# Two matmul layers of a graph network in three blocks of 418 columns in place of four of 314

## The reference

```python
h = jnp.maximum(_layernorm(x, axis=-1), 0.0)
agg = jax.ops.segment_sum(h[src], dst, num_segments=N)
z = (1.0 + eps) * h + agg
z = jax.nn.relu(batch_norm(z @ W1 + b1, g1, be1))      # 512 -> 1024, statistics over the nodes
z = jax.nn.relu(batch_norm(z @ W2 + b2, g2, be2))      # 1024 -> 512
x = x + h + z
```

## Time and profile before

| | us |
|---|---|
| median of 3 runs | 1132.43 |
| lowest and highest | 1132.26 and 1136.16 |
| the profiled execution: its own time | 1133.7 |
| its span, first to last instruction | 1131.7 |
| PE busy | 1063.5 (94%) |
| ACT, DVE, POOL busy | 896.6, 871.2, 656.5 |
| mean granted TensorE clock | 0.986 of full speed |

### The profile page before, as it was taken

The page is one execution under the profiler, slowest core; times in us unless marked ns, Lnnn a source line. Parts: engine busy times, 40 slices in busy tenths (PEclk is TensorE's granted clock), DMA queues, the critical chain, the costliest instruction groups (busy, mean ns, idle before and its releaser), DMA issues.

```text
span 1131.7 us, 18418 instructions
## 1 busy us (share of the span) xinstructions
PE 1063.5 (94%) x5689; PEld 896.5 (79%) x5690; DVE 871.2 (77%) x1529; ACT 896.6 (79%) x1134; POOL 656.5 (58%) x549
## 2 busy tenths in 40 slices
PE   3676999998999999999999999999999999999897
PEld 1124889997888888888888888888888888888695
DVE  7998536535425388888898998998888888888686
ACT  5995845524513699999999999999999999999584
POOL 6765323002155486776888888888876677660217
PEclk9998999998999999999999999999999999999899
DMA  2004820301165386666666666666666666661002
GB/s 102 8 1 115 147 75 1 121 1 47 75 215 121 81 188 146 138 136 139 130 137 140 133 133 145 132 140 130 140 138 133 136 139 134 134 130 38 1 1 91
DMA packets 61086, 121.39 MB, mean 107 GB/s; under 512 B 7851, under 2 KB 18348, under 8 KB 60918
## 3 DMA queue, kind: packets, MB, share of 16 engines
q0 software_dynamic: 38048, 87.58, 38.1%
q1 hardware_dynamic: 22998, 33.32, 8.9%
HBM read 107.82 MB, written 7.80 MB: 102 GB/s over the span
## 4 chain that ended last, share of the span: by engine, by line
PE 86%; DVE 9%; ACT 2%; issue 2%; DVEq 1%; POOL 0%; ACTq 0%; POOLq 0%
PE banks L1033 12%; PE banks L1028 12%; PE banks L1029 12%; PE banks L933 10%; PE banks L1013 7%; PE banks L1050 6%; PE banks L1007 6%; PE banks L976 5%; PE banks L856 4%; PE banks L995 4%; DVE edge_counts L1688 4%; PE banks L1026 3%; PE banks L1110 2%; DVE key_onehot L1635 1%; PE banks L910 1%
## 5 line engine op out<-in xcount | busy, mean ns | idle before, releaser
L682 POOL DMA_INDIRECT gather_pq<-q_table,dst x157 | 295.4, 1882 | 56.8 <-issue 47.5
L674 POOL DMA_INDIRECT gather_pq<-p_table,src x157 | 173.5, 1105 | 138.7 <-PE banks L1013 85.5
L1028 PE MATMUL banks<-w_lo,h_hi 128*128 128x512 f32 x620 | 241.5, 390 | 0.0
L1029 PE MATMUL banks<-w_hi,h_hi 128*128 128x512 f32 x620 | 241.3, 389 | 0.0
L1033 PE MATMUL banks<-w_hi,h_lo 128*128 128x512 f32 x620 | 166.2, 390 | 0.0
L1029 PEld LDWEIGHTS banks<-w_hi,h_hi 128*128 128x128 f32 x620 | 116.4, 188 | 24.8
L1033 PEld LDWEIGHTS banks<-w_hi,h_lo 128*128 128x128 f32 x620 | 116.4, 188 | 24.2
L1984 DVE SCALAR_TENSOR_TENSOR h_full<-mish_work,banks 128x512 f32<-128x512 f32 (+1 forms) x154 | 98.5, 681 | 46.6 <-ACT mish_work L1337 43.4
L1028 PEld LDWEIGHTS banks<-w_lo,h_hi 128*128 128x128 f32 x620 | 116.5, 188 | 22.0
L2009 DVE SCALAR_TENSOR_TENSOR message<-mish_work,banks 128x1024 f32<-128x1024 f32 x78 | 95.3, 1222 | 8.7 <-ACT mish_work L1361 0.7
L1325 ACT ACTIVATE mish_work<-banks 128x1024 f32<-128x1024 f32 (+1 forms) x77 | 78.6, 1021 | 26.3 <-PE banks L1013 26.3
(11 more groups left out here) (267 smaller groups left out, 2677.5 us busy)
## 6 DMA issues: line engine op xcount, KB each, us to landing
edge_attr<-in_edge_attr_t SPq DMA_DIRECT2D x79, 128.0 KB, 3.5
x_nodes<-h_hi POOLq DMA_DIRECT2D x10, 256.0 KB, 13.3
x_nodes<-h_lo POOLq DMA_DIRECT2D x10, 256.0 KB, 7.9
p_table<-p_stage SPq DMA_DIRECT2D x10, 256.0 KB, 2.0
q_table<-agg_nodes SPq DMA_DIRECT2D x10, 256.0 KB, 3.0
gather_pq<-p_table,src POOLq DMA_INDIRECT x157, 3.9
gather_pq<-q_table,dst POOLq DMA_INDIRECT x157, 5.0
x_nodes<-in_x SPq DMA_DIRECT2D x3, 768.0 KB, 6.7
```

Of the source, the lines that this page charges most:

```text
L674: nc.gpsimd.indirect_dma_start(GP[:, 2 * j + k, :], None, p_tab[:, :], bass.IndirectOffsetOnAxis(ap=SRC[:, 2 * s + k:2 * s + k + 1], axis= ...
L682: nc.gpsimd.indirect_dma_start(GP[:, 2 * j + k, :], None, q_tab[:, :], bass.IndirectOffsetOnAxis(ap=DST[:, 2 * s + k:2 * s + k + 1], axis= ...
L1028: pe.matmul(at, h_high(s, j)[:, c, e], W2_LO[:, c, :], start=False, stop=False)
L1029: pe.matmul(at, h_high(s, j)[:, c, e], W2_HI[:, c, :], start=False, stop=False)
```

## The change

The first network's products go over 3 blocks of 418 columns (1254 in all). The update of the second network keeps 4 blocks of 314 under the names `UBLOCKS` and `UBW`. Three places depend on the number of blocks without being about width: PE's inner split of a tile's blocks becomes (0, 1) and (1, 3), where it was (0, 2) and (2, 4); ACT's `between` stands behind block `BLOCKS // 2`, now 1; `FREE`, the number of banks that are free at the start, becomes 3.

```diff
-BLOCKS = 4
-
-BW = -(-NODES // (2 * BLOCKS)) * 2
+
+
+BLOCKS, UBLOCKS = 3, 4
+BW, UBW = (-(-NODES // (2 * n)) * 2 for n in (BLOCKS, UBLOCKS))
 NW = BLOCKS * BW
-assert NODES <= NW <= NP
+assert NODES <= NW <= UBLOCKS * UBW <= NP
...
-        FREE = 4
+        FREE = BLOCKS
         MM_2 = BLOCKS * KH
         MM_PQ = MM_2 + BLOCKS * KD
         MM_UP = MM_PQ + 2 * NT
-        MM_U = MM_UP + BLOCKS * KD
+        MM_U = MM_UP + UBLOCKS * KD
...
                 for o in range(1, on):
-                    for first, end in ((0, BLOCKS // 2), (BLOCKS // 2, BLOCKS)):
+                    for first, end in ((0, 1), (1, BLOCKS)):
                         with pe.Fori(first, end) as b:
                             pe.wait_ge(mm_moved, base + BLOCKS * o + b + 1)
                             for k in range(kn):
...
-                nodes = slice(b * BW, (b + 1) * BW)
+                nodes = slice(b * UBW, (b + 1) * UBW)
...
-            for b in range(BLOCKS):
+            for b in range(UBLOCKS):
                 for o in range(KD):
```

More of the change, by code:

```diff
@@ L174, in gnn_kernel @@
         IOTA, _ = sb("iota", [P, NP])
-        XWORK_0, _ = sb("mish3_work_0", [P, 2, BW], at=iota_at)
-        XWORK_1, _ = sb("mish3_work_1", [P, 2, BW], at=b2_at)
+        XWORK_0, _ = sb("mish3_work_0", [P, 2, UBW], at=iota_at)
+        XWORK_1, _ = sb("mish3_work_1", [P, 2, UBW], at=b2_at)
         XWORK = (XWORK_0[:, :, :], XWORK_1[:, :, :])
@@ L323, in gnn_kernel @@
         W3B_HI, W3B_LO = W3_HI[:, 0, :, :], W3_LO[:, 0, :, :]
[L324 to L327, removed]
+        UP_0, _ = sb("u_part_0", [P, 6, UBW], at=wa_at + 4 * KD * DIM)
+        UP_1, _ = sb("u_part_1", [P, 6, UBW], at=wb_at + 4 * KD * DIM)
+        UP_2, _ = sb("u_part_2", [P, 4, UBW], at=rows_at)
+        assert 4 * 6 * UBW <= 4 * KD * DIM and 4 * 4 * UBW <= 4 * 3 * DIM
         UT, _ = sb("u_t", [P, KD, NP], at=t1_at)
@@ L745, in u_high @@
                 b, q = n // UPAIRS, n % UPAIRS
-                at = (slice(2 * q, 2 * q + 2), slice(b * BW, (b + 1) * BW))
+                at = (slice(2 * q, 2 * q + 2), slice(b * UBW, (b + 1) * UBW))
                 pool.wait_ge(u_ready, n + 1)
@@ L757, in _ @@
             pool.wait_ge(tr_done, TR_AG + NT)
-            for n in range(UPAIRS * BLOCKS):
+            for n in range(UPAIRS * UBLOCKS):
                 u_high(n)
@@ L1023, in z2 @@
                     else:
-                        pe.wait_ge(up_moved, BLOCKS * KD)
+                        pe.wait_ge(up_moved, UBLOCKS * KD)
                     pe.wait_ge(h_hi, s + 1)
@@ L1082, in _ @@
                         pe.wait_ge(up_moved, n - 3)
-                    u_terms(Z2[:, n % 4, 0:BW], W3A_HI, W3A_LO, HT_HI, HT_LO, o, b)
+                    u_terms(Z2[:, n % 4, 0:UBW], W3A_HI, W3A_LO, HT_HI, HT_LO, o, b)
                     if n in Z1_BEHIND:
@@ L1103, in y_product @@
                     pe.wait_ge(y_moved, nt - 3)
-                nodes = slice(nt * P, min((nt + 1) * P, NW))
-                last_block = (nodes.stop - 1) // BW
+                nodes = slice(nt * P, min((nt + 1) * P, UBLOCKS * UBW))
+                last_block = (nodes.stop - 1) // UBW
                 for k in range(KD):
@@ L1114, in u_product @@
             def u_product(b, q):
-                pe.wait_ge(ag_lo, -(-(b + 1) * BW // P))
+                pe.wait_ge(ag_lo, -(-(b + 1) * UBW // P))
                 if b > 0:
@@ L1120, in u_product @@
                 for o in (2 * q, 2 * q + 1):
-                    u_terms(Z2[:, o, 0:BW], W3B_HI, W3B_LO, AG_HI, AG_LO, o, b)
+                    u_terms(Z2[:, o, 0:UBW], W3B_HI, W3B_LO, AG_HI, AG_LO, o, b)
             def ag_t(nt):
@@ L1134, in _ @@
             ag_t(9)
-            for b in range(1, BLOCKS):
+            for b in range(1, UBLOCKS):
                 for q in range(UPAIRS):
@@ L1396, in _ @@
                         act.wait_ge(rows_used, 2 * NT)
-                    nc.scalar.activation(u_part(b, o)[:, 0, :], Z2[:, n % 4, 0:BW], ACT.Identity, bias=COLS[:, CB3 + o:CB3 + o + 1]).then_inc(up_moved, 1)
+                    nc.scalar.activation(u_part(b, o)[:, 0, :], Z2[:, n % 4, 0:UBW], ACT.Identity, bias=COLS[:, CB3 + o:CB3 + o + 1]).then_inc(up_moved, 1)
                     for s, first in enumerate(Z1_BEHIND):
@@ L1469, in _ @@
             u_inverse(0)
-            for n in range(1, UPAIRS * BLOCKS):
+            for n in range(1, UPAIRS * UBLOCKS):
                 u_mish(n)
@@ L2098, in u_at @@
                 b, q = n // UPAIRS, n % UPAIRS
-                return slice(2 * q, 2 * q + 2), slice(b * BW, (b + 1) * BW)
+                return slice(2 * q, 2 * q + 2), slice(b * UBW, (b + 1) * UBW)
             def u_start(n):
@@ L2105, in u_start @@
                 dve.wait_ge(mm_done, MM_U + KD * b + 2 * q + 2)
-                nc.vector.tensor_tensor(UT[:, o, nodes], Z2[:, o, 0:BW], u_part(b, 2 * q, 2), ALU.add).then_inc(u_bias, 1)
+                nc.vector.tensor_tensor(UT[:, o, nodes], Z2[:, o, 0:UBW], u_part(b, 2 * q, 2), ALU.add).then_inc(u_bias, 1)
             def u_bound(n):
@@ L2160, in _ @@
             ag_low(9)
-            for n in range(2, UPAIRS * BLOCKS):
+            for n in range(2, UPAIRS * UBLOCKS):
                 u_end(n - 2)
```

## The result

The change makes the kernel slower: 1150.39 us median of 3 runs (1148.62 to 1150.61), against 1132.43, so 18.0 us more by the medians. The forecast was 1147.1, range 1141 to 1152. The profiled execution took 1150.39 us, with a span of 1148.3, 16.6 more than that of before (which lay 1.3 us above the median of its own kernel).

The account below looks back on a forecast made before the run. PE, busy 94% of the span, was taken to bound the kernel. Savings of 1.4 and 1.3 us against losses of 0.1, 10.1, 4.8 and 2.4 gave +14.7 on 1132.43, so 1147.1 us, range 1141 to 1152.

Parts of the forecast that it names:

- handover, first three k of product 2: Start of product 2, tile 0: DVE sets the pace, so no saving, and ACT's wider last move adds 0.1 us.
- Three new waits: Product 2, tiles 0 to 2: PE's transposes wait 3.35 us each for ACT's apply behind block 0, +10.1 us.
- The clock: Behind each new wait in product 2 the granted clock falls to half for one stretch, 1.6 us each, +4.8.
- The saving: Fewer, wider matmuls save fixed cost: 1.4 us in product 1 and 1.3 in product 2.
- 384 matmuls at 144.5 ns become 288 at 187.7: Product 1: 55.5 us of matmuls become 54.1, a saving of 1.4 us.
- the second point of the line: 512-column matmuls at 226.6 ns; with 314 columns they gave 0.415 ns per column plus 14, so 187.7 at 418.
- The 0.5 us that was estimated by the 2.5 ns: Products 1 and 2: alternative saving from 192 fewer matmuls at the skill's fixed cost; not used in the sum.
- The late end of DVE: End of product 2: ten layer-norm statistics make DVE 2.2 us late for the last block; last apply +2.4 us.
- What costs nothing: Three banks, fewer DVE and ACT operations, and the unchanged update add nothing; one possible bank wait up to 1 us.
- The bank wait of product 1: Product 1, near 181.5 us: 1 us of cover expected; a wait showing there would be a sign of error.
- The sum: Whole kernel: -1.4 - 1.3 + 0.1 + 10.1 + 4.8 + 2.4 = +14.7 us, giving 1147.1.

Follow-up runs that it names:

- e1: Changed kernel with product 2's transposes behind the first two of three blocks; 1135.87 us, ratio 1.002 to the kernel before.
- e2: Kernel before, four blocks of 314, with product 2's transposes behind the first block alone; 1148.11 us, ratio 1.0116.
- e12: Changed kernel with twelve further DVE operations ahead of the edge loop and nothing else; 1149.32 us, ratio 1.0144.
- e3: Changed kernel with 14 unread matmuls ahead of each of three transpose groups inside product 2; 1147.3 us, ratio 1.0119.
- e6: Kernel before with unread matmuls in its own waits, around the last transposes, ahead of P and at the edge attributes; 1130.47 us, ratio 0.9967.
- e5: Three blocks, transposes behind two, columns left out or repeated to vary matmul width; only start distances read, 145.3 ns at 314 columns, 216.7 at 480.
- e11: Three blocks with transposes behind two, late layer-norm statistics, filled waits and twelve more DVE operations, against the kernel before; 1130.69 us, ratio 0.9976.

## Why the prediction was right or wrong

Against the profiled execution of before, the 16.6 us of span are made up so (the rows add up to 16.5, each being rounded):

| from where to where | forecast | measured |
|---|---|---|
| start of product 1 | 0 | +0.4 |
| matmuls of product 1 | -1.4 | -0.2 |
| handover, first three k of product 2 | +0.1 | +0.1 |
| matmuls of product 2 | -1.3 | -0.3 |
| three waits | +10.1 | +10.1 |
| low clock behind them | +4.8 | +3.2 |
| end of product 2, PE's last matmul to the last apply | +2.4 | +2.25 |
| P's first tile | 0 | +0.3 |
| no fall of the clock behind the edge attributes | 0 | -1.6 |
| edge loop | 0 | +2.4 |
| rest | 0 | -0.2 |

**Three new waits: right,** in place, cause and size. From the start of the last matmul of block 0 to the transposes it was 3.54 us by forecast; measured, ACT's move begins at 231.41 and PE goes on at 234.66, which with the 0.39 ahead is 3.64, and 3.54 and 3.55 the other two times. 10.1 is worked out from the three, less 0.19 each. e1 and e2 show the cause from both sides.

**The clock: right in mechanism, too large by a third in this run.** The step took one stretch for each wait; behind the first the clock stayed up. Each of the others cost 1.6 as forecast. It differs between executions with the same waits: in e2's it fell behind all three, in e12's behind the first and third. e3 shows that PE's idling is what brings it about. Here the rule of the Trainium skill (TensorE: Matmul & The Clock Gate, section "HAM oscillation — how this bites in real kernels") that the prediction set beside the rows (idle gaps let the gate go back to half speed) agrees with the trace at two of the three waits and not at the first, of 3.29 us, behind which the clock stayed at 1.00. e3 and e6 bear it out from the other side: behind the filled waits no fall came.

**The saving: the step that failed.** The term "384 matmuls at 144.5 ns become 288 at 187.7" was mis-sized: it is 191.9 in product 1 and 191.1 to 192.2 in three stretches of 36 matmuls in product 2, and the saving of both is 0.5 us, not 2.7. The fault was to take the second point of the line from the 512-column matmuls of P and Q: e5 has all widths from 352 up above that line, within products 1 and 2. The 0.5 us that was estimated by the 2.5 ns of the Trainium skill (TensorE: Matmul & The Clock Gate, section "Wait — 56ns, not 53.3ns?") comes near only by chance. At 2.4 GHz 314 columns are 130.8 ns and 418 are 174.2, so the rows have 14 ns beside the columns at 314 and 18 at 418, and not 2.5.

**The late end of DVE: right,** 2.25 for 2.4; the last apply begins 4.90 us after ACT's last move, where it was 2.67 (284.92 to 289.82, and 271.46 to 274.13).

**What costs nothing: nearly.** The bank wait of product 1 was looked for at 181.5 and shows as two starts 0.08 us late each at 182.24 and 182.51. The prediction had named such a wait as a sign of being wrong; it came, but as 0.16 us in all. What it had at nothing without a word is the edge loop, and that grew by 2.4 us, the largest thing the prediction did not see. The twelve operations of e11 and e12 take it away.

**The sum: near in part by luck.** The saving (2.2 us too large) and the edge loop (2.4) err the same way and would have put the span 4.6 us above the forecast. That only 1.9 are left is the clock's doing, -1.6 in product 2 and -1.6 at the edge attributes, and neither was foreseen for this execution.

## What to carry to other kernels

When a loop over blocks is cut differently, look at everything that is placed by counting blocks: work "behind the first half" moved here from two blocks to one, and its cover of 0.25 us became a wait of 3.3. Compare the cover with the chain it covers, from the end of the tile and not in blocks.

A wait of PE of some 3 us costs its length and can cost about half as much again in clock. Where PE must wait anyway, matmuls that nothing reads and that end before the wait does cost nothing here, and gave 3.5 us in the kernel before.

If a loop that was not touched changes its time, look in the view of waits for "issue" at the first operation of its body, and try some empty operations ahead of it before looking for a cause in the data.

## What the runs showed of the hardware that I had not expected

- The first operation of DVE's loop body can start 0.24 us behind the last one, in place of 0.09, in every pass, by what stands ahead of the loop: 8.3 to 9.1 us of such gaps in 35 or 36 passes. The edge loop is 1.6 to 2.5 us longer with them, which is 0.04 to 0.07 us for each pass. They went with twelve further operations ahead of the loop and were untouched by moving the tiles.
- The granted clock does not fall behind every wait of the same length: of the changed kernel's three waits of 3.1 to 3.3 us two brought it down, of e2's three all; a wait of 2.59 us brought it down in the kernel before, and one of 2.6 not in the changed one. The low stretches in product 2 lasted 3.4 us each.
- From 314 to 480 columns the cost of a matmul from start to start has no step: 145.3 ns at 314, 180.8 at 400, 189.2 at 416, 190.3 to 192.2 at 418, 216.7 at 480 (e5, e1 and the changed kernel).
